# Token maxima reduced by VectorE straight from the inner values, and the rounding offset written into the banks ahead of the output products

## The reference, cut to what matters

```
x = x + 0.5 * ffn(layernorm(x))        # phase 1 of the kernel
x = x + ssm_and_cfc(layernorm(x))      # in between
x = x + 0.5 * ffn(layernorm(x))        # phase 2

def ffn(x):                            # D = 1024, hidden 4096
    h = bit_linear(x, w1)              # x rounded to 8 bits per token, w1 to -1, 0, 1
    h = silu(depthwise_conv1d(h))      # three taps along the tokens
    return bit_linear(h, w2)

def act_quant(x):                      # inside bit_linear
    scale = 127.0 / clip(max(abs(x), axis=-1), 1e-05)
    return clip(round(x * scale), -128, 127) / scale
```

## Time and profile before

| | |
|---|---|
| median of 3 runs | 1722.78 us |
| the profiled execution | 1719.35 us |
| its span on the slowest core | 1717.8 us |
| PE busy | 1279.5 us, 74% |
| DVE busy | 1172.6 us, 68% |
| ACT busy | 958.1 us, 56% |
| POOL busy | 642.6 us, 37% |
| mean granted TensorE clock, median core of either die | 0.946 |

### The profile page before, as it was taken

One profiled execution on the slowest core, in us unless ns is written; L12 is line 12 of the kernel. 1 busy time (PEld: TensorE's weight loads), 2 busy tenths in 40 slices (PEclk: granted clock), 3 DMA queues, 4 the chain that ended last, 5 costly groups with the idle time before them and its releaser, 6 DMA issues. The chain is left out here.

```text
span 1717.8 us, 29950 instructions; the slowest of 8 cores (1714.5 to 1717.8 us)
## 1 busy us (share of the span) xinstructions
PE 1279.5 (74%) x9089; PEld 860.0 (50%) x9107; DVE 1172.6 (68%) x2126; ACT 958.1 (56%) x1428; POOL 642.6 (37%) x668
## 2 busy tenths in 40 slices
PE   0000087698898998998659987357699999998999
PEld 0000065465565665654348866135465655655644
DVE  4898568687687776774266666458776776777741
ACT  0426167766776766674246654146666666665651
POOL 0000322555756746547500024221633535334332
PEclk9999999899999999999869999579999999998999
DMA  9590210212122221114120000111111111200111
GB/s 290 176 334 4 62 38 13 62 37 51 38 50 62 62 51 38 51 38 118 55 50 2 2 1 2 52 59 50 50 50 64 61 50 56 81 26 26 50 38 62
DMA packets 35765, 105.66 MB, mean 62 GB/s; under 512 B 4756, under 2 KB 14100, under 8 KB 34584
## 3 DMA queue, kind: packets, MB, share of 16 engines
q1 hardware_dynamic: 24568, 95.08, 16.7%
q0 software_dynamic: 11040, 8.66, 3.5%
HBM read 84.58 MB, written 25.70 MB: 64 GB/s over the span
## 5 line engine op out<-in xcount | busy, mean ns | idle before, releaser
L587 PE MATMUL bank<-xqT,w1q 128*128 128x258 bf16 (+1 forms) x4352 | 575.4, 277 | 111.2 <-DVE y L891 110.6
L587 PEld LDWEIGHTS bank<-xqT,w1q 128*128 128x128 fp8e4 x4352 | 417.4, 100 | 277.4 <-issue 149.3
L608 PE MATMUL bank<-w2q,q 128*128 128x512 fp8e4 x2112 | 535.2, 383 | 0.0
L921 DVE SCALAR_TENSOR_TENSOR y<-bank,convws,y 128x256 f32<-128x256 f32 (+1 forms) x544 | 256.4, 471 | 270.3 <-ACT y L738 269.2
L1055 POOL TENSOR_TENSOR y<-y,Rb 128x1024 f32<-128x1024 f32 (+1 forms) x136 | 322.8, 2403 | 179.3 <-ACT Rb L763 179.3
L738 ACT ACTIVATE y<-bank,convbs,convws 128x256 f32<-128x256 f32 (+1 forms) x544 | 293.1, 551 | 165.0 <-PE bank L587 161.3
L608 PEld LDWEIGHTS bank<-w2q,q 128*128 128x128 f16 x2112 | 206.1, 98 | 166.1 <-issue 7.9
L891 DVE SCALAR_TENSOR_TENSOR y<-bank,convws,y 128x256 f32<-128x256 f32 (+1 forms) x544 | 253.8, 467 | 0.1
L689 ACT ACTIVATE y<-y 128x1024 f32<-128x1024 f32 (+1 forms) x136 | 139.9, 1029 | 149.5 <-DVE y L891 149.3
L832 DVE TENSOR_TENSOR M<-M,ab 128x1024 f32<-128x1024 f32 (+1 forms) x119 | 199.4, 1676 | 2.2 <-ACT ab L701 2.2
L711 ACT ACTIVATE q<-y,qoff 128x1024 f16<-128x1024 f32 (+1 forms) x136 | 151.8, 1117 | 65.8 <-POOL y L1055 62.3
(11 more groups left out here) (159 smaller groups left out, 1328.7 us busy)
## 6 DMA issues: line engine op xcount, KB each, us to landing
raw<-w1T SPq DMA_DIRECT2D x8, 2048.0 KB, 35.2
raw<-w2T SPq DMA_DIRECT2D x8, 2048.0 KB, 17.8
xg<-xall SPq DMA_DIRECT2D x18, 512.0 KB, 5.2
x1t<-xall SPq DMA_DIRECT2D x17, 512.0 KB, 4.1
basebuf<-x1t SPq DMA_DIRECT2D x17, 512.0 KB, 3.1
xg<-basebuf SPq DMA_DIRECT2D x16, 512.0 KB, 4.6
x2buf<-xg SPq DMA_DIRECT2D x16, 512.0 KB, 2.9
x1t<-x2buf SPq DMA_DIRECT2D x16, 512.0 KB, 4.3
```

The costliest lines, as they stand in the source:

```text
L587: mm = pe.matmul(pA[n % 4][:, 0:tw + 2], w1q[:, c, k * P:(k + 1) * P], xqT[j % 3][:, c, 0:tw + 2], start=c == 0, stop=c == DC - 1)
L608: pe.matmul(pB[e % 2][:], q[:, qs, kh, :], w2q[:, kh, 512 * h:512 * h + 512], start=kh == 0, stop=False)
L921: dve.scalar_tensor_tensor(v, pA[n % 4][:, 0:tw], convws[:, 3 * k:3 * k + 1], v, ALU.mult, ALU.add).then_inc(conv1_done, 1)
```

## The change

DVE no longer needs absolute values from ACT. It reduces `y` itself: a `tensor_reduce` with absolute value over the slot index, in five parts (slots 0 to 7, 8 to 15, 16 to 23, 24 to 27, 28 to 31), each into a slot of its own of `M`, which now has five. The read is rearranged so that the innermost step goes from slot to slot, 1024 bytes. The parts stand at k = 11, 19, 27, 31 and at k = 3 of the next stage. The fold is one reduction over the five slots of `M`.

The correction by -1536 times the column sums is made once per phase (`offsets`, two matmuls of 512 columns) and kept in SBUF as `offs`. Before each accumulation ACT writes the half row of `offs` into the bank (`begin_b`, at k = 27 for the first of a tile and at k = 3, 11, 19 for the others), and all 32 matmuls of the accumulation add onto it. PE waits for that write (`begun`) where it waited for the evacuation.

```
+PARTS = ((0, 8), (8, 16), (16, 24), (24, 28), (28, 32))
+PART_SLOT = {11: 0, 19: 1, 27: 2, 31: 3}
...
-    M = at('M', O, [P, 4, T])
+    M = at('M', O, [P, 5, T])
...
-    ab_ = {1: at('ab1', E + 23104, [P, 4, T]), 2: at('ab2', E + 26880, [P, 4, T])}
+    offs = {1: at('offs1', E + 23104, [P, D]), 2: at('offs2', E + 26880, [P, D])}
...
# PE
+        def offsets():
+            if ph == 1:
+                pe.wait_ge(s2_done, 2)
+            for h in range(2):
+                mm = pe.matmul(pB[h][:], negc[:], S2[:, 512 * h:512 * h + 512], start=True, stop=True)
+            mm.then_inc(offs_mm, 1)
...
+                if k == 4 and j == 2 - ph:
+                    offsets()
...
                     if k % 8 == 0:
-                        if e >= 2:
-                            pe.wait_ge(evac_done, e - 1)
-                        elif ph == 1:
-                            pe.wait_ge(s2_done, 2)
+                        pe.wait_ge(begun, e + 1)
...
-                        pe.matmul(pB[e % 2][:], q[:, qs, kh, :], w2q[:, kh, 512 * h:512 * h + 512], start=kh == 0, stop=False)
+                        mm = pe.matmul(pB[e % 2][:], q[:, qs, kh, :], w2q[:, kh, 512 * h:512 * h + 512], start=False, stop=kh == HC - 1,
+                                       skip_group_check=True)
                     if k % 8 == 7:
-                        pe.matmul(pB[e % 2][:], negc[:], S2[:, 512 * h:512 * h + 512], start=False, stop=True).then_inc(b_done, 1)
+                        mm.then_inc(b_done, 1)
...
# ACT: absolute() and its calls at k = 2 and k = 6, 10, 14, ... are gone
+        def begin_b(t, i):
+            if not 0 <= t < nt or i >= 2 * halves(ph, t):
+                return
+            e = 4 * t + i
+            if e >= 2:
+                act.wait_ge(evac_done, e - 1)
+            if e == 0:
+                act.wait_ge(offs_done, 2)
+            act.activation(pB[e % 2][:], offs[ph][:, 512 * (i % 2):512 * (i % 2) + 512], AF.Identity).then_inc(begun, 1)
...
+                if k == 3:
+                    begin_b(j - 2, 1)
+                if k == 6 and j == 2 - ph:
+                    for h in range(2):
+                        act.wait_ge(offs_mm, 1)
+                        act.activation(offs[ph][:, 512 * h:512 * h + 512], pB[h][:], AF.Identity).then_inc(offs_done, 1)
+                if k == 11:
+                    begin_b(j - 2, 2)
+                if k == 19:
+                    begin_b(j - 2, 3)
+                if k == 27:
+                    begin_b(j - 1, 0)
...
# DVE
-            dve.tensor_tensor(M[:, :, 0:w], M[:, :, 0:w], ab_[ph][:, :, 0:w], ALU.max).then_inc(max_done, 1)
+        def part_max(t, i):
+            a, z = PARTS[i]
             w = width(ph, t)
+            s0 = (HC * t + a) % YR
+            dve.wait_ge(silu_done, 8 * t + z // 4)
+            if t:
+                dve.wait_ge(fold_done, t)
+                if i == 4:
+                    dve.wait_ge(scaled_done, 8 * t)
+            dve.tensor_reduce(M[:, i, 0:w], y[:, s0:s0 + z - a, 0:w].rearrange('p k t -> p t k'), AX.X, ALU.max,
+                              apply_absolute_value=True).then_inc(max_done, 1)
...
         def fold(t):
-            dve.tensor_tensor(M[:, 0:2, 0:w], M[:, 0:2, 0:w], M[:, 2:4, 0:w], ALU.max).then_inc(fold_half, 1)
-            dve.tensor_tensor(rep[:].rearrange('p g t -> p (g t)')[:, 0:w], M[:, 0, 0:w], M[:, 1, 0:w], ALU.max).then_inc(fold_done, 1)
+            dve.tensor_reduce(rep[:].rearrange('p g t -> p (g t)')[:, 0:w], M[:, :, 0:w].rearrange('p k t -> p t k'),
+                              AX.X, ALU.max).then_inc(fold_done, 1)
```

More of the change, by code:

```diff
@@ L126, in build_nc @@
     MB = O
-    M = at('M', O, [P, 4, T])
+    M = at('M', O, [P, 5, T])
     O += 4 * T * 4
+    Rb = at('Rb', O, [P, 2 * P])
+    O += 1024
     rep = at('rep', O, [P, 2, P])
-    O += 1024
-    Rb = at('Rb', O, [P, 2 * P])
     O += 1024
@@ L239, in build_nc @@
     silu_done = sem('silu_done')
-    abs_done = sem('abs_done')
     max_done = sem('max_done')
-    fold_half = sem('fold_half')
     fold_done = sem('fold_done')
@@ L254, in build_nc @@
     s2_done = sem('s2_done')
+    offs_mm = sem('offs_mm')
+    offs_done = sem('offs_done')
+    begun = sem('begun')
     pstat_part = sem('pstat_part')
@@ L747, in ffn_act @@
                     silu(j - 1, 7)
-                if k == 2 and 1 <= j <= nt:
-                    absolute(j - 1, 7)
+                if k == 3:
[10 more added lines that the diff above has]
+                    begin_b(j - 1, 0)
                 if k == 4 and j >= 1 and 2 * j + 3 < ng:
@@ L753, in ffn_act @@
                     silu(j, (k - 5) // 4)
-                if k >= 6 and k % 4 == 2 and j < nt:
-                    absolute(j, (k - 6) // 4)
                 if k == 11 and ph == 1 and 3 <= j and 2 * (j - 3) + 1 < 17:
@@ L825, in amax_x @@
                 dve.reciprocal(psc[0:n, a + 1:a + 2], psc[0:n, a:a + 1]).then_inc(pamax_done, 1)
[L827 to L830, removed]
+        def part_max(t, i):
+            a, z = PARTS[i]
             w = width(ph, t)
-            dve.tensor_tensor(M[:, :, 0:w], M[:, :, 0:w], ab_[ph][:, :, 0:w], ALU.max).then_inc(max_done, 1)
+            s0 = (HC * t + a) % YR
[6 more added lines that the diff above has]
+                              apply_absolute_value=True).then_inc(max_done, 1)
         def fold(t):
             w = width(ph, t)
-            dve.wait_ge(max_done, 7 * t + 7)
-            dve.tensor_tensor(M[:, 0:2, 0:w], M[:, 0:2, 0:w], M[:, 2:4, 0:w], ALU.max).then_inc(fold_half, 1)
-            dve.wait_ge(fold_half, t + 1)
+            dve.wait_ge(max_done, 5 * t + 5)
             if t:
                 dve.wait_ge(repT_done, t)
-            dve.tensor_tensor(rep[:].rearrange('p g t -> p (g t)')[:, 0:w], M[:, 0, 0:w], M[:, 1, 0:w], ALU.max).then_inc(fold_done, 1)
+            dve.tensor_reduce(rep[:].rearrange('p g t -> p (g t)')[:, 0:w], M[:, :, 0:w].rearrange('p k t -> p t k'),
+                              AX.X, ALU.max).then_inc(fold_done, 1)
         def y_scale(t):
@@ L932, in ffn_dve @@
                 if k == 3 and 1 <= j <= nt:
-                    take_max(j - 1, 7)
+                    part_max(j - 1, 4)
                     fold(j - 1)
@@ L938, in ffn_dve @@
                     stat_x(2 * j + 4)
-                if k >= 11 and k % 4 == 3 and j < nt:
-                    take_max(j, (k - 7) // 4)
+                if k in PART_SLOT and j < nt:
+                    part_max(j, PART_SLOT[k])
                 if k == 8 and 0 <= t < nt:
```

## The result

| | before | after |
|---|---|---|
| median of the runs | 1722.0 us | 1742.4 us |
| profiled execution, longest span | 1717.8 us | 1742.1 us |
| instructions on that core | 29950 | 29449 |

The ratio is 1.0121, with a 95% interval of 1.0107 to 1.0135: slower, by less than the 2% that I called a difference. The forecast was 1737 us, range 1655 to 1780. It held; its working holds less well.

What follows compares the result with a forecast made beforehand. PE's list plus 4 to 6 us of waiting, chiefly for DVE's right tap, bounds a full stage. Twelve items sum to +15 on the profiled 1719.35 us, so 1734; 3.4 for the median gives 1737 us, range 1655 to 1780.

Steps and rivals of the forecast that it cites:

- The price: DVE's new strided reductions: 1.84 ns an element, taken from the cast with the like step; ends 1.08 and 3.69.
- Item 11: ACT: 136 absolute values go, 66 bank writes and four copies come; nothing on the path either way.
- DVE never became the bound: Rival: eight-slot parts on DVE at 3.69 ns an element, 73.8 us of DVE a stage; 1850 us, chance 0.13.
- the writes were never late: Rival: ACT's writes come late and PE waits at each accumulation; 1750 to 1790 us, chance 0.07.
- the free step: Rival: a wide step costs DVE's reductions nothing, 1.08 ns an element; -55, 1668 us, chance 0.34.
- Item 1: PE: 66 correcting matmuls go, four come, 0.21 us each where PE is mostly the bound; -12 us.
- Item 2: POOL freed of the maxima: its power step loses 0.96 us in 11 stages, scaling starts earlier; -11 us.
- Item 3: Stage 6 of phase 2: blocked maximum becomes 3.78 us, PE's 7.34 us idle and half-clock stretch go; -10 us.
- Items 4 to 9: DVE's parts and fold at k = 27, 19, 31, 3, 11, 19: +8, +3, +4, +8, +7 and +3, +5 us.
- item 4: DVE at k = 27: the part takes 3.78 us for the maximum's 3.06, in 11 stages; +8 us.
- Item 10: Stages 0 and 1 of both phases: DVE's parts replace maxima, ACT loses absolute values; +2.3 us a stage, +9.
- Item 12: The tail: 0.5 more between last silu and scales, and one wait for column sums in stage 1; +1 us.

Runs made afterwards that it cites:

- the column version: Kernel before with offsets in the banks; ACT writes absolute values into rows of six, DVE reduces five neighbours, no two-input maxima: 1719.0 us, ratio 0.9996.
- the version with one-input maxima: Kernel before with DVE's in-place two-input maximum replaced by a contiguous one-input reduction of ab alone, running maximum lost: 1657.6 us, ratio 0.9639.

## Why the prediction was right, and where it wasn't

**The price** (between 1.08 and 3.69, 1.84 taken) was right, 1.79, with luck in it: a plain copy with the same step costs 1.1, so the cast was not a measure of strided reads in general. Item 11 was right (no write late), and so were the rivals' fates: DVE never became the bound, the writes were never late, and the free step gave the total that its rival had said, 1665 for 1668. The step as a whole was put at 1737 - 1668 = 69 us and is 76. DVE's work per tile was added up wrongly: three parts of 3.77, two of 1.89 and the fold of 2.36 are 17.4 us, not 15.6, against 13.1 before. No item of the sum uses the 15.6. The trace has 4.7 to 4.9 us more a stage.

**Item 1** (-12) is somewhat high: the offsets bring 9 us on the old maxima (6 to 12 by the interval) and 6 on the new. In the full stages of phase 1 their share is close to nothing, and in the column version so is the whole.

**Item 2** (-11) was mis-sized, and this is the largest error. The lock costs 62 us in the kernel before. I read one of POOL's victims, the power step, and one of the maxima's places. Even that step was misread: it takes 1.53 us in five stages of phase 1 only, and beside the maximum of k = 23, not that of k = 27; in phase 2 a neighbour loses as much in five more. The earlier trace rows had the clue: 112 maxima at a mean of 1715 ns against the 1.22 of the earlier trace rows are 55 us of stretching, of which the places named in the text explain some 29 (11 at k = 27 by 1.84, one of 9). In the changed kernel k = 22 to 27 of phase 1 takes 11.2 us in stage 4, 14.7 before, where I had allowed 0.96. The relief alone is 2.3 of these 3.5 us: the version with one-input maxima needs 12.5 there. The rest is likely that the slots ahead now run 4.2 us later and wait less for POOL.

**Item 3** (-10) brought 3.5 in the trace. The wait of 7.34 us went, but one of 2.74 came earlier in the stage, at k = 12, behind a DVE step with two SBUF inputs that meets the scaling:

```profile
1583.18 1.85 DVE L839 TENSOR_TENSOR psc<-psc,pcs 2x1 f32<-2x1 f32 x1 [0.46 <-DVE psc L835]
...
1585.97 1.26 PE L597 MATMUL bank<-xqT,w1q 128*128 128x258 bf16 x8 [2.74 <-DVE y L911]
```

One element, 1.85 us, and 0.15 to 0.16 in the kernel before: the same lock, by its look. The step is as long or longer in five other versions.

**Items 4 to 9**, stage 4 as the example, in us between the left taps (item 1's 0.6 to 0.8 a stage is left out of the forecasts):

| slots | phase 1 | forecast | phase 2 | forecast |
|---|---|---|---|---|
| 0 to 8 | 12.9 to 14.8 | +1.3 | 14.2 to 14.8 | 0 |
| 8 to 16 | 16.0 to 16.9 | +1.1 | 16.2 to 16.4 | +0.6 |
| 16 to 22 | 10.0 to 11.4 | +0.9 | 11.7 to 11.9 | +0.6 |
| 22 to 27 | 14.7 to 11.2 | -1.0 | 11.9 to 10.9 | -1.0 |
| 27 to 0 | 14.3 to 14.9 | +1.4 | 14.6 to 15.0 | +0.7 |

The signs are right, and the sizes within 0.7 except in the fourth row of phase 1. What I didn't see is that item 4 was a choice of place, not a price: at k = 27 the part stands between a late tap and the statistics for which PE waits, and two slots later that wait is gone, with 47 of the 76 us that hang on the step.

**Item 10** (+9, with the stages' share of the others +14) is +22.4, on the median core +19.0. These stages have no output products to hide DVE behind; the parts make PE stand, and its granted clock falls with that. In stages 0 and 1 of both phases PE was at half clock 35 us before and 71 us after (over the eight cores 24 to 41 and 49 to 71). One by one they are longer by 4.5, 4.7, 8.8 and 4.4 us, and "by more than 6 us" was my own sign of being wrong: stage 0 of phase 2 passed it, on the median core too (6.9). I priced the DVE time alone. How much of the error is clock, no run separates: with the part at k = 29 stage 1 of phase 1 still has 20 us at half clock and is 4.2 us shorter.

**Item 12** can't be told from the rest (-1.8 from the last stage on).

So that the total was near is luck: the misses have opposite signs. The full stages of phase 1 came 10 us cheaper than forecast, with POOL's relief put too small; the early stages came 8 us and stage 6 of phase 2 came 7 us dearer.

## What to carry to other kernels

Before pricing an operation, compare the mean of its group with its shortest instance, and go through every place where it is longer: that difference is another engine's work, and it counts on both sides. A long step on an engine with idle time is priced by what stands behind it in its list; first move it behind the steps that others wait for, then judge it. A reduction of fp32 values over an outer index took 1.6 times as long as soon as neighbours were 16 bytes apart, so a cheaper count of instructions can be a dearer read; and when the step was moved to the writer, ACT's write took twice as long.

## Of the hardware, not expected

- ACT's absolute value of 1024 values takes 1.05 us to contiguous places and 2.05 us where neighbours go 24 bytes apart (128 instances).
- A VectorE step with two SBUF inputs of one element waits for GpSimd as a large one does (1.85 us).
- A single SBUF input does not keep every VectorE step free, as it keeps the reduction and the tap. A `tensor_scalar` on two values a partition takes 0.17 us alone; in the changed kernel it took 0.89 to 0.99 us in eight stages, and ended with GpSimd's centring of the input group (timeline of the changed kernel). In the kernel before, this happened in phase 1 alone:

```profile
435.99 1.20 POOL L1022 TENSOR_SCALAR xg<-xg,pco 128x1024 f32<-128x1024 f32 x1 [0.18 <-POOL pco L1013]
436.30 0.92 DVE L873 TENSOR_SCALAR ysc<-amx 128x2 f32<-128x2 f32 x1
```

- GpSimd's step with a single SBUF input is locked too: 1.04 us alone, 1.82 beside the maximum.
- Reductions with runs spread by 16 or 32 bytes take 3.77 to 3.81 us, by 64 bytes and more 3.57 to 3.59: the nearest dear steps are the dearest.
